# A graph network on one Trainium2 core: in the first edge sweep the rank row is loaded to one partition and spread by TensorE

## The chip, the cores and the metric

The kernel runs on one core of one Trainium2 chip, as a single launch. The metric is device time in microseconds (us) of that core, lower being better. TensorE is called PE in the profile, VectorE DVE, ScalarE ACT, GpSimd POOL and SyncE SP.

## The reference, cut to what matters

Four message-passing layers run over one graph of 6250 nodes with 128 features and 106250 edges, which are sorted by receiver (`dst`). Each is followed by a residual and a layer norm. Only the first layer is touched by the change:

```python
msg_in = jnp.concatenate([h[src], h[dst], w[:, None]], axis=1)
msg = jax.nn.relu(msg_in @ W1 + b1) @ W2 + b2
agg = jax.ops.segment_max(msg, dst, num_segments=n)
```

`h[src] @ W1[:128]` and `h[dst] @ W1[128:256]` are made once per node, as two tables in HBM; what is left for each edge is to fetch a row of each, add them and `w * W1[256]`, apply relu, multiply by `W2`, and take the maximum over the edges of one receiver.

## The kernel before, in words

An **edge sweep** goes over the edges in 208 blocks (`NB`) of 512 edges (`EB`), each of four tiles of 128 (`CT`). A **node phase** lies between two sweeps. `edge_phase(k)` is the first sweep with k = 1 and the two last with k = 4 and 5; `relation_phase` is the second (k = 2) and `attention_phase` the third. Only `edge_phase(1)` changes in what it does.

In the first sweep a block goes through the engines like this.

- **SP** (`load`) waits for a free `meta` buffer (`e_meta_free`, four buffers), then issues three transfers from HBM: `meta` (L1071), `recv` (L1076, 256 KB, the receivers' rows) and the edge weights (L1083, 2 KB). The `meta` transfer reads two rows of 512 bf16 values, the **rank row** (for each edge, which of the receiver rows in its tile it belongs to) and the **bar row** (what restarts the running maximum at a new receiver), and writes each of them to all 128 partitions: 256 KB.
- **POOL** (`gather`) issues four indirect transfers (L1040), one per tile, that fetch 128 rows of the joint table by `src`. It waits for a free gather buffer (`e_gath_free`) and for the store of half of that buffer's earlier content (`factor_out`).
- **DVE** (`same_receiver`, L1228) compares the rank row with a column of ranks and so makes the 0/1 matrix `same`, which spreads one receiver's row over its edges.
- **PE** (`senders`) waits for `recv`, `same` and the gather, then makes the sum in `pre_ps`: one matmul for the weight (L1120), and per tile one for the senders (L1123) and one for the receivers (L1124). `message` multiplies the hidden layer by `W2` (L1132), `turn_back` transposes the result of the scan (L1142).
- **ACT** (`hidden`) first issues the store of the factor half (L1168), then applies relu (L1171); it makes the gather's indices (L1156), and `keep_rows` frees `scan`, copies the transposed rows (L1184) and stores them (L1190).
- **DVE** (`reduce`, L1247) takes the running maximum over the block with `meta[s][:, 2, :]`, the bar row, and then frees the `meta` buffer, for which SP is waiting.

Each engine runs its pieces in an order written out by hand with `steps(engine, NB, SLOTS, (lag, piece), ...)`: in step i it does each piece for block i - lag, in the order given. Before, PE's step is `senders(i)`, `message(i-1)`, `turn_back(i-3)`; DVE's is `same_receiver(i)`, `reduce(i-2)`; ACT's is `hidden(i-4)`, `indices(i)`, `keep_rows(i-7)`; SP's is `load(i)`, which runs up to four blocks ahead.

The second sweep, `relation_phase`, already has the form that the change brings to the first: its `meta` rows go to one partition (L1292), `rank_row` on PE spreads the rank row with a bf16 matmul against a row of ones (L1315), and DVE compares out of PSUM (L1408).

Of the kernel before, what the change touches and what calls it, by code (L numbers as in the profile page):

```python
# [17 lines left out]
P = 128  # L18
# [5 lines left out]
EB = 512  # L24
CT = EB // P
NB = -(-E // EB)
# [8 lines left out]
SLOTS = 4  # L35
# [6 lines left out]
ALU = mybir.AluOpType  # L42
# [30 lines left out]
def gnn_program(nc, a, out):  # L73
# [8 lines left out]
    def sem(name):  # L82
        return ctx.enter_context(nc.semaphore(name))
# [4 lines left out]
    with ctx:  # L88
# [129 lines left out]
        t_er_free = sem("t_er_free"); t_cb_free = sem("t_cb_free"); t_gath_free = sem("t_gath_free")  # L218
        e_idx_free = sem("e_idx_free")
        e_rank = sem("e_rank"); e_rank_free = sem("e_rank_free")  # L220
        e_go = sem("e_go"); e_go_free = sem("e_go_free")

        def part(q, s, unroll, n):
# [781 lines left out]
        def edge_phase(k):  # L1005
# [2 lines left out]
            table, width = (joint_d, 2 * F) if k == 1 else (send_d, F)  # L1008
            landed = {1: joint, 2: factor}.get(k, gath)
            marks = {1: (1, 3), 2: (0, 2)}.get(k, (0, 1))  # L1010
            pre_ps, msg_ps, back_ps = bank[0:2], bank[2:4], bank[4:6]
            before = started["edge"]
            firsts_before, scatters = started["firsts"], started["scatter"]

# [2 lines left out]
            with nc.Block() as block:  # L1017
# [34 lines left out]
                @block.sync  # L1052
                def _(sp):
                    if expands:

                        sp.wait_ge(n_scat_all, 1)
                        sp.sem_inc(n_scat_all, -1)
                        sp.wait_ge(firsts_got, 16 * (firsts_before + TC))
                        by_tile = first_d.rearrange("(b p c) f -> b p c f", p=P, c=CT)
                        for c in range(TC):  # L1060
                            n = P if c < TC - 1 else TL
                            sp.dma_start(by_tile[c * P // CT:(c * P + n) // CT, 0, :, :], firsts[c // CT][0:n, c % CT, :]).then_inc(n_first_out, 16)
                        sp.wait_ge(n_first_out, 16 * TC)
                        sp.sem_inc(n_first_out, -16 * TC)

                    def load(q, s):

                        sp.wait_ge(e_meta_free, 1)
                        sp.sem_inc(e_meta_free, -1)
                        lo, hi = marks  # L1070
                        sp.dma_start(meta[s][:, lo:hi, :], meta_d[lo:hi, part(q, s, SLOTS, EB)].partition_broadcast(P)).then_inc(meta_in[s], 16)  # L1071
                        if expands:

                            sp.wait_ge(e_recv_free, 1)
                            sp.sem_inc(e_recv_free, -1)
                            sp.dma_start(recv[s][:, :, :], first_d[part(q, s, SLOTS, EB), :].rearrange("(p c) f -> p c f", c=CT)).then_inc(recv_in[s], 16)  # L1076
                            if k == 2:

                                sp.wait_ge(e_gath_free, 1)
                                sp.sem_inc(e_gath_free, -1)  # L1080
                                sp.dma_start(factor[s][:, :, :], factor_rows_d[part(q, s, SLOTS, EB), :].rearrange("(p c) f -> p c f", c=CT)).then_inc(factor_in[s], 16)
                            if k == 1:
                                sp.dma_start(wrow[s][:, :], weight_d[:, part(q, s, SLOTS, EB)]).then_inc(recv_in[s], 16)  # L1083

                    def store(q, s):

                        sp.wait_ge(e_rows, 1)
                        sp.sem_inc(e_rows, -1)
                        sp.dma_start(scan_d[part(q, s, SLOTS, EB), :].rearrange("(p c) f -> p c f", c=CT), rows[s][:, :, 0:F]).then_inc(stored[s], 16)

                    if expands:
                        steps(sp, NB, SLOTS, (0, load), *[(5, store)] * (k == 2))

                @block.tensor
                def _(pe):
                    def senders(q, s):
                        if expands:

                            pe.wait_ge(recv_in[s], 32 if k == 1 else 16)
                            pe.sem_inc(recv_in[s], -(32 if k == 1 else 16))  # L1100

                            pe.wait_ge(e_same, 1)
                            pe.sem_inc(e_same, -1)

                        pe.wait_ge(e_pre_free, 1)
                        pe.sem_inc(e_pre_free, -1)
                        if k == 2:

                            pe.wait_ge(factor_in[s], 16)
                            pe.sem_inc(factor_in[s], -16)  # L1110
                        else:
                            pe.wait_ge(gathered[s], (q + 1) * (16 * CT) + 16 * CT * rounds * before)
                        b, g = pre_ps[s % 2], landed[s]
                        if k >= 4:
                            for c in range(CT):
                                ins = pe.transpose(b[:, c * P:(c + 1) * P], g[:, c, 0:F], ident[:, :])  # L1116
                            ins.then_inc(e_pre, 1)
                            return
                        if k == 1:
                            pe.matmul(b[:, :], w1w[:, :], wrow[s][:, :], start=True, stop=False)  # L1120
                        for c in range(CT):
                            o = b[:, c * P:(c + 1) * P]
                            pe.matmul(o, g[:, c, 0:F], ident[:, :], start=k != 1, stop=False)  # L1123
                            ins = pe.matmul(o, recv[s][:, c, :], same[s % 2][:, c, :], start=False, stop=k != 1 or c == CT - 1)  # L1124
                        ins.then_inc(e_pre, 1)

                    def message(q, s):
                        pe.wait_ge(e_hid, 1)
                        pe.sem_inc(e_hid, -1)
                        pe.wait_ge(e_msg_free, 1)  # L1130
                        pe.sem_inc(e_msg_free, -1)
                        pe.matmul(msg_ps[s % 2][:, :], w2[:, :], hid[s % 2][:, :], start=True, stop=True).then_inc(e_msg, 1)  # L1132

                    def turn_back(q, s):

                        pe.wait_ge(e_scan, 1)
                        pe.sem_inc(e_scan, -1)

                        pe.wait_ge(e_back_free, 1)
                        pe.sem_inc(e_back_free, -1)  # L1140
                        for c in range(CT):
                            ins = pe.transpose(back_ps[s % 2][:, c * P:(c + 1) * P], scan[s % 2][:, c * P:(c + 1) * P], ident[:, :])  # L1142
                        ins.then_inc(e_back, 1)

                    steps(pe, NB, SLOTS, (0, senders), *[(1, message)] * (k == 1), (3 if expands else 2, turn_back))

                @block.scalar
                def _(act):
# [62 lines left out]
                def _(v):  # L1211
# [9 lines left out]

                    def same_receiver(q, s):

                        v.wait_ge(meta_in[s], 16)
                        v.sem_inc(meta_in[s], -16)
                        v.wait_ge(e_same_free, 1)
                        v.sem_inc(e_same_free, -1)
                        v.tensor_tensor(same[s % 2][:, :, :], meta[s][:, 1, :].rearrange("p (c e) -> p c e", e=P),  # L1228
                                        rank_cols[:, part(q, s, SLOTS, CT)].unsqueeze(2).to_broadcast([P, CT, P]), ALU.is_equal).then_inc(e_same, 1)

                    def reduce(q, s):
                        if k >= 4:

                            v.wait_ge(meta_in[s], 16)
                            v.sem_inc(meta_in[s], -16)
                        v.wait_ge({1: e_msg, 2: e_hid}.get(k, e_pre), 1)
                        v.sem_inc({1: e_msg, 2: e_hid}.get(k, e_pre), -1)
                        if k == 1:
                            v.sem_inc(e_hid_free, 1)
                        if k >= 4:  # L1240
                            v.sem_inc(e_gath_free, 1)
                            v.sem_inc(e_idx_free, 1)
                        v.wait_ge(e_scan_free, 1)
                        v.sem_inc(e_scan_free, -1)  # L1244
                        src = {1: msg_ps, 2: hid}.get(k, pre_ps)[s % 2][:, :]
                        go_on = meta[s][:, 2 if k == 1 else 0, :]
                        chain(v.tensor_tensor_scan(scan[s % 2][:, :], go_on, src, scan[1 - s % 2][:, EB - 1:EB],  # L1247
                                                   ALU.add if k == 1 else ALU.mult, ALU.max if k == 1 else ALU.add))
                        v.sem_inc({1: e_msg_free, 2: e_hid_free}.get(k, e_pre_free), 1)
                        v.sem_inc(e_meta_free, 1)  # L1250
                        v.sem_inc(e_scan, 1)
# [551 lines left out]
```

## Time and profile before

| | |
|---|---|
| three timed runs | 6587.62, 6593.26 (median), 6595.1 us |
| profiled execution | 6596.86 us, of which 6595.1 us are its span |
| busy shares of the span | PE 56%, PE weight load 43%, DVE 38%, ACT 21%, POOL 59% |
| first sweep | from 396 to 1530 us of the span |
| in the first sweep | PE 999, DVE 411, ACT 309, POOL 844 us busy of 1134; DMA share 0.94 |

Busy shares over the whole span say little here, since the six stages have different limits. The first sweep is one stage of some 1130 us, and the change is to be read from that stretch alone. The DMA share is the mean busy share of the core's 16 DMA engines. Indirect transfers are issued by POOL, and an issue counts as POOL's busy time.

### The profile page before, as it was taken

To read this page: it belongs to the slowest core of one execution; us is meant where nothing else is said; L and a number is where in the kernel's file an instruction comes from. 1 tells how busy PE (TensorE), PEld (TensorE's weight loads), DVE (VectorE), ACT (ScalarE), POOL (GpSimd) and SP (SyncE) were. 2 spreads that over 40 slices of the span, in tenths; PEclk is the share of its full clock that TensorE was granted. 3 is DMA by queue.
4 is the path that set the end of the run, shared out by engine and by line. 5 is a ranking of instruction groups with operands and counts; after the bars stand their busy time and mean duration, and the time that the engine had idled before them with its cause. 6 is when DMAs were issued, how large, how long until landed. Compare 5 with 4: busy or idle time off the path is not lost. (4 is left out here: it accounts for less than half of the span.)

```text
span 6595.1 us, 101052 instructions
## 1 busy us (share of the span) xinstructions
PE 3682.2 (56%) x19907; PEld 2827.0 (43%) x19907; DVE 2495.9 (38%) x4067; ACT 1392.2 (21%) x3059; POOL 3886.5 (59%) x3936
## 2 busy tenths in 40 slices
PE   1258888896587777636666564233333343333334
PEld 1145565564465555435555554123323332332332
DVE  4223333334344444525655555422222212222224
ACT  0012222222122232212222222111111111111111
POOL 0467777776200000667777774577777757777775
PEclk9679999998799999767878777555555565555556
DMA  9369999993355555256656563344544434444452
GB/s 343 123 193 293 291 296 292 298 297 105 122 182 182 186 182 171 81 124 171 168 156 168 156 169 103 92 126 125 127 126 125 126 86 126 125 127 126 125 127 75
DMA packets 1080339, 1090.67 MB, mean 165 GB/s; under 512 B 128353, under 2 KB 867622, under 8 KB 1076854
## 3 DMA queue, kind: packets, MB, share of 16 engines
q1 hardware_dynamic: 398532, 393.02, 20.3%
q10 hardware_dynamic: 546204, 390.09, 19.1%
q0 software_dynamic: 135456, 306.11, 18.5%
q14 instruction: 117, 0.96, 0.0%
q8 instruction: 30, 0.49, 0.0%
HBM read 662.62 MB, written 427.19 MB: 165 GB/s over the span
## 5 line engine op out<-in xcount | busy, mean ns | idle before, releaser
L1040 POOL DMA_INDIRECT gath<-sender_table,idx x1664 | 1657.6, 996 | 547.4 <-issue 376.0
L1247 DVE TENSOR_TENSOR_SCAN scan<-meta,scan,bank 128x512 f32<-128x512 bf16 x624 | 798.6, 1280 | 2086.1 <-DVEq L1244 2083.0
L1116 PE MATMUL bank<-ident,gath 128*128 128x128 f32 x1664 | 464.1, 434 | 1367.3 <-DMA gath<-sender_table,idx 1367.3
L1463 POOL DMA_INDIRECT gath<-attention_table,idx x832 | 852.3, 1024 | 349.3 <-issue 226.7
L1040 POOL DMA_INDIRECT gath<-joint_table,idx x832 | 850.3, 1022 | 273.6 <-issue 213.0
L1116 PEld LDWEIGHTS bank<-ident,gath 128*128 128x128 f32 x1664 | 297.7, 217 | 1533.4 <-DMA gath<-sender_table,idx 1533.4
L682 POOL COPY idx<-end_i 128x4 int32<-128x4 int32 (+1 forms) x65 | 13.5, 207 | 1040.5 <-POOLq L681 1040.3
L1184 ACT ACTIVATE rows<-bank 128x512 f32<-128x512 f32 x624 | 372.7, 597 | 1101.7 <-ACTq L1183 1059.1
L1142 PE MATMUL bank<-ident,scan 128*128 128x128 f32 x2496 | 570.1, 374 | 5.0 <-PEq L1140 5.0
L1142 PEld LDWEIGHTS bank<-ident,scan 128*128 128x128 f32 x2496 | 471.7, 203 | 132.0 <-issue 132.0
L1123 PE MATMUL bank<-ident,gath 128*128 128x128 f32 x1664 | 374.8, 310 | 0.0
L1329 PE MATMUL bank<-ident,gath 128*128 128x128 f32 x1664 | 350.5, 294 | 23.7 <-PEq L1325 12.0
L1124 PE MATMUL bank<-same,recv 128*128 128x128 f32 x1664 | 357.2, 300 | 0.0
L1514 PE MATMUL bank<-recv,same 128*128 128x4 f32 x1664 | 229.0, 261 | 222.8 <-PEq L1512 215.6
L1123 PEld LDWEIGHTS bank<-ident,gath 128*128 128x128 f32 x1664 | 279.3, 211 | 161.6 <-issue 161.6
L1514 PEld LDWEIGHTS bank<-recv,same 128*128 128x128 f32 x1664 | 223.4, 208 | 255.9 <-issue 255.9
L1120 PE MATMUL bank<-small,w1w 1*128 1x512 f32 x416 | 237.1, 650 | 165.3 <-DMA gath<-joint_table,idx 113.8
L1422 DVE TENSOR_TENSOR_SCAN scan<-bank,scan,hid 128x512 f32<-128x512 f32 x208 | 266.8, 1283 | 159.3 <-DVEq L1421 159.3
L1156 ACT ACTIVATE idx<-src_cols 128x4 int32 (+1 forms) x624 | 127.8, 205 | 876.9 <-ACTq L1194 772.5
L1171 ACT ACTIVATE hid<-bank,b 128x512 f32<-128x512 f32 x208 | 143.0, 687 | 739.8 <-ACTq L1170 667.0
L1329 PEld LDWEIGHTS bank<-ident,gath 128*128 128x128 f32 x1664 | 263.1, 199 | 80.9 <-issue 80.9
L1124 PEld LDWEIGHTS bank<-same,recv 128*128 128x128 f32 x1664 | 285.6, 215 | 0.0
(245 smaller groups left out, 6065.8 us busy)
## 6 DMA issues: line engine op xcount, KB each, us to landing
recv<-receiver_rows SPq DMA_DIRECT2D x624, 256.0 KB
scan_rows<-rows ACTq DMA_DIRECT2D x624, 256.0 KB
attention_scan_rows<-rows ACTq DMA_DIRECT2D x208, 264.0 KB
receiver_rows<-gath ACTq DMA_DIRECT2D x26, 2048.0 KB, 11.2
meta<-edge_meta SPq DMA_DIRECT2D x208, 256.0 KB
factor_rows<-gath ACTq DMA_DIRECT2D x208, 256.0 KB
gath<-factor_rows SPq DMA_DIRECT2D x208, 256.0 KB
scan_rows<-rows SPq DMA_DIRECT2D x208, 256.0 KB
```

The source lines that it names most:

```text
L1040: pool.indirect_dma_start(out=landed[s][:, c, 0:width], out_offset=None, in_=table[:, :], in_offset=bass.IndirectOffsetOnAxis(ap=idx[s][:, ...
L1116: ins = pe.transpose(b[:, c * P:(c + 1) * P], g[:, c, 0:F], ident[:, :])
L1120: pe.matmul(b[:, :], w1w[:, :], wrow[s][:, :], start=True, stop=False)
L1123: pe.matmul(o, g[:, c, 0:F], ident[:, :], start=k != 1, stop=False)
L1124: ins = pe.matmul(o, recv[s][:, c, :], same[s % 2][:, c, :], start=False, stop=k != 1 or c == CT - 1)
L1142: ins = pe.transpose(back_ps[s % 2][:, c * P:(c + 1) * P], scan[s % 2][:, c * P:(c + 1) * P], ident[:, :])
L1184: ins = act.activation(rows[s][:, :, 0:F], back_ps[s % 2][:, :].rearrange("p (c f) -> p c f", f=F), ACT.Copy)
L1247: chain(v.tensor_tensor_scan(scan[s % 2][:, :], go_on, src, scan[1 - s % 2][:, EB - 1:EB], ALU.add if k == 1 else ALU.mult, ALU.max if k = ...
L1329: pe.matmul(o, factor[s][:, c, :], ident[:, :], start=True, stop=False)
L1422: chain(v.tensor_tensor_scan(scan[s % 2][:, :], go_ps[s % 2][:, :], hid[s % 2][:, :], scan[1 - s % 2][:, EB - 1:EB], ALU.mult, ALU.add))
L1463: pool.indirect_dma_start(out=gath[s][:, c, :], out_offset=None, in_=att_d[:, :], in_offset=bass.IndirectOffsetOnAxis(ap=idx[s][:, c:c + 1 ...
L1514: ins = pe.matmul(er_ps[:, c * HEADS:(c + 1) * HEADS], same[s % 2][:, c, :], recv[s % SLOTS][:, c, 0:F:HID], start=True, stop=True)
```

## The change

The rank row no longer goes to all partitions. SP loads it to partition 0, in a transfer of its own of 1 KB, and the bar row in a second broadcast transfer of 128 KB with a semaphore of its own (`bar_in`). PE spreads the rank row into PSUM (banks 6 and 7, `rank_ps`) with one bf16 matmul per block, in front of `senders` of the block before, so that PE's other pieces come one step later. DVE compares out of PSUM, with the running maximum waiting for `bar_in`.

```diff
+        bar_in = [sem(f"bar_in{s}") for s in range(SLOTS)]
...
-                        sp.dma_start(meta[s][:, lo:hi, :], meta_d[lo:hi, part(q, s, SLOTS, EB)].partition_broadcast(P)).then_inc(meta_in[s], 16)
+                        sp.dma_start(meta[s][0:1, lo:lo + 1, :], meta_d[lo:lo + 1, part(q, s, SLOTS, EB)].unsqueeze(0)).then_inc(meta_in[s], 16)
+                        sp.dma_start(meta[s][:, lo + 1:hi, :], meta_d[lo + 1:hi, part(q, s, SLOTS, EB)].partition_broadcast(P)).then_inc(bar_in[s], 16)
...
+                    def rank_row(q, s):
+                        pe.wait_ge(meta_in[s], 16)
+                        pe.sem_inc(meta_in[s], -16)
+                        pe.wait_ge(e_rank_free, 1)
+                        pe.sem_inc(e_rank_free, -1)
+                        pe.matmul(rank_ps[s % 2][:, :], ones_row[:, :], meta[s][0:1, 1, :], start=True, stop=True).then_inc(e_rank, 1)
...
-                    steps(pe, NB, SLOTS, (0, senders), *[(1, message)] * (k == 1), (3 if expands else 2, turn_back))
+                    if expands:
+                        steps(pe, NB, SLOTS, (0, rank_row), (1, senders), (2, message), (4, turn_back))
+                    else:
+                        steps(pe, NB, SLOTS, (0, senders), (2, turn_back))
...
-                        v.wait_ge(meta_in[s], 16)
-                        v.sem_inc(meta_in[s], -16)
+                        v.wait_ge(e_rank, 1)
+                        v.sem_inc(e_rank, -1)
                         v.wait_ge(e_same_free, 1)
                         v.sem_inc(e_same_free, -1)
-                        v.tensor_tensor(same[s % 2][:, :, :], meta[s][:, 1, :].rearrange("p (c e) -> p c e", e=P),
-                                        rank_cols[:, part(q, s, SLOTS, CT)].unsqueeze(2).to_broadcast([P, CT, P]), ALU.is_equal).then_inc(e_same, 1)
+                        chain(v.tensor_tensor(same[s % 2][:, :, :], rank_ps[s % 2][:, :].rearrange("p (c e) -> p c e", e=P),
+                                              rank_cols[:, part(q, s, SLOTS, CT)].unsqueeze(2).to_broadcast([P, CT, P]), ALU.is_equal))
+                        v.sem_inc(e_rank_free, 1)
+                        v.sem_inc(e_same, 1)
...
+                        if k == 1:
+                            v.wait_ge(bar_in[s], 16)
+                            v.sem_inc(bar_in[s], -16)
```

## Rows read from the trace of the kernel before

**Rows 1.** Windows: busy us of each engine, PE clock, DMA share, GB/s.

```profile
600.00:800.00 200.00, 177.68 (x899) 117.99 (x898) 73.55 (x75) 55.13 (x111) 152.75 (x150) 0.93 0.95 294
2000.00:2600.00 600.00, 475.79 (x3071) 356.32 (x3070) 275.23 (x279) 179.88 (x280) 0.00 (x0) 0.97 0.59 183
```

**Rows 2.** Groups of instructions by line, first sweep, window 600 to 1400 us.

```profile
L1040 POOL DMA_INDIRECT gath<-joint_table,idx x600 | 614.1, 1024 | 187.4 <-issue 155.2 <-POOLq L1038 13.0 <-POOLq L1034 11.6
...
L1228 DVE TENSOR_TENSOR same<-meta,rank_cols 128x512 f32<-128x512 bf16 x150 | 104.1, 694 | 190.7 <-DVEq L1227 162.6 <-ACTq L1164 14.8 <-DVEq L1225 9.2
```

**Rows 3.** The page's costliest groups: the gathers of the whole first sweep.

```profile
L1040 POOL DMA_INDIRECT gath<-joint_table,idx x832 | 850.3, 1022 | 273.6 <-issue 213.0 <-POOLq L1038 32.6 <-POOLq L1034 16.2
```

**Rows 4.** Instructions of line 1040, first sweep, then last sweeps (ns: min/median/max).

```profile
L1040 POOL DMA_INDIRECT gath<-joint_table,idx x823: 992/998/1512, 399.5 to 1510.3; - x165
...
L1040 POOL DMA_INDIRECT gath<-sender_table,idx x1199: 992/997/1013, 4799.8 to 6466.8; - x200
```

**Rows 5.** Timeline: start, length; gathers of POOL beside comparisons of DVE.

```profile
405.99 1.19 POOL L1040 DMA_INDIRECT gath<-joint_table,idx  x1 [0.30 <-issue]
...
1013.56 0.69 DVE L1228 TENSOR_TENSOR same<-meta,rank_cols 128x512 f32<-128x512 bf16 x1 [1.46 <-DVEq L1227]
1013.72 1.40 POOL L1040 DMA_INDIRECT gath<-joint_table,idx  x1 [0.30 <-issue]
...
1508.92 1.09 POOL L1040 DMA_INDIRECT gath<-joint_table,idx  x1 [0.30 <-issue]
```

**Rows 6.** Waits, window 600 to 1400 us: engine, who for whom, us, times, longest.

```profile
PEld bank L1120 <- DMA gath<-joint_table,idx: 104.2, 91, 2.8
```

**Rows 7.** DMA queue of SP, window 600 to 1400 us: packets, MB, share.

```profile
q1 hardware_dynamic: 62471, 78.64, 31.6%
```

**Rows 8.** Timeline: one turn of a block, from senders to the next load.

```profile
1009.56 1.12 PE L1120 MATMUL bank<-small,w1w 1*128 1x512 f32 x2
...
1013.92 0.69 ACT L1171 ACTIVATE hid<-bank,b 128x512 f32<-128x512 f32 x1 [2.48 <-ACTq L1170]
...
1015.23 1.28 DVE L1247 TENSOR_TENSOR_SCAN scan<-meta,scan,bank 128x512 f32<-128x512 bf16 x1 [0.98 <-DVEq L1244]
...
1016.98 0.38 SPq L1071 DMA_DIRECT2D meta<-edge_meta  x1
```

**Rows 9.** Timeline: the first and the last pair of senders and load.

```profile
409.09 1.22 PE L1120 MATMUL bank<-small,w1w 1*128 1x512 f32 x1
...
417.77 0.40 SPq L1071 DMA_DIRECT2D meta<-edge_meta  x1
...
1500.61 0.69 PE L1120 MATMUL bank<-small,w1w 1*128 1x512 f32 x1
...
1507.71 0.38 SPq L1071 DMA_DIRECT2D meta<-edge_meta  x1
```

**Rows 10.** Timeline, second sweep: first and last load of rows, and PE behind it.

```profile
1724.18 0.73 SPq L1292 DMA_DIRECT2D meta<-edge_meta  x1
...
1726.37 0.58 PE L1315 MATMUL bank<-meta,ones_row 1*128 1x512 bf16 x1 [42.61 <-PEq L1314]
...
2609.83 0.63 SPq L1292 DMA_DIRECT2D meta<-edge_meta  x1
...
2611.92 0.37 PE L1315 MATMUL bank<-meta,ones_row 1*128 1x512 bf16 x1 [0.81 <-PEq L1314]
...
2612.38 0.46 PE L1329 MATMUL bank<-ident,gath 128*128 128x128 f32 x2
```

**Rows 11.** Timeline, first sweep: a comparison that waited for its broadcast rows.

```profile
1022.73 0.37 SPq L1071 DMA_DIRECT2D meta<-edge_meta  x1
...
1028.32 0.69 DVE L1228 TENSOR_TENSOR same<-meta,rank_cols 128x512 f32<-128x512 bf16 x1 [1.27 <-DMA meta<-edge_meta]
```

**Rows 12.** Instructions of line 1408, second sweep: the comparison out of PSUM.

```profile
L1408 DVE TENSOR_TENSOR same<-bank,rank_cols x104: 691/692/693, 1727.2 to 2604.3; 128x512 f32<-128x512 f32 x104
```

More of the change, by code:

```diff
@@ L1010, in edge_phase @@
             marks = {1: (1, 3), 2: (0, 2)}.get(k, (0, 1))
-            pre_ps, msg_ps, back_ps = bank[0:2], bank[2:4], bank[4:6]
+            pre_ps, msg_ps, back_ps, rank_ps = bank[0:2], bank[2:4], bank[4:6], bank[6:8]
             before = started["edge"]
```

## The prediction

> **What bounds the first sweep now.** I read the windows by stage first. In the steady part of the first sweep PE is busy 178 of 200 us, POOL 153, and the DMA engines 0.95 of the time [rows 1]. Three resources are near their end, so the busy shares do not name the bound. The groups by line do: between 600 and 1400 us POOL issues 600 gathers, 150 blocks, so a block takes 800 / 150 = 5.333 us; POOL's instructions are busy for 614.1 us and idle 187.4 [rows 2]. Nearly every gather has the same 0.30 us in front of it [rows 5], 180 us for 600, which is issue cost and no wait. Only some 6 of 800 us are left as waits for another engine. POOL's row of gathers is the bound.
>
> How low can it go? The median gather takes 998 ns [rows 4], so four of them with 0.30 each are 4 x 1.298 = 5.19 us per block. The step is 0.14 us longer. One part of that is in the gathers' own length: they average 1024 ns here, while in the last sweeps the longest of 1199 is 1013 [rows 4]. Over the sweep that is 832 x (1.022 - 0.998) = 20 us [rows 3, 4]. The timeline says where it lies. In the first sweep 82 of the 832 gathers last over 1.02 us (first and last: [rows 5]), and each begins just ahead of or inside a comparison L1228 on DVE, as at 1013.72, 0.16 us into one, with 1.40 us [rows 5]. None of the 669 gathers that begin away from one is long. So POOL is held by the comparison, not by the full DMA queues.
>
> The Trainium skill has a rule for this (page "SBUF — State Buffer", section "Who interferes with whom"): a DVE instruction with two SBUF inputs contends with a GpSimd instruction that reads SBUF, since its second input comes through the shared read interface; one with at most one SBUF input does not. The trace agrees as far as it goes. By that rule the 20 us go entirely once one input lies in PSUM.
>
> PE has some room: its first matmul of a block waits for the gather 104.2 us in 150 blocks [rows 6], 0.69 us each, so its own work is about 5.33 - 0.69 = 4.64 us.
>
> **The change, part by part.**
>
> Removed: 128 KB per block minus 1 KB of transfers. SP's queue moves 78.64 MB in 150 blocks [rows 7], 0.52 MB each, and each of the other two streams about as much, so some 8% of all bytes go. As DMA is not what the gathers wait for, this is worth nothing directly. It makes the queues shorter; the waits of POOL outside the steady part could shrink: 273.6 us idle over 832 gathers [rows 3] less 832 x 0.30 leaves 24 us, of which 6 are in the steady part [rows 2]. I count none of the other 18 us, and keep 5 of them for the range.
>
> The comparison: out of PSUM it takes 692 ns [rows 12] against 694 now [rows 2]. No cost. Its other effect is the gain above, if the mechanism is what I take it for: up to 20 us, or 0.10 us per block. The second sweep has no gathers beside its comparison, so no row shows this directly; the bounds are 0 and 20 us, and I take 20, because only gathers that meet L1228 are long, and the scans (one operand in PSUM) leave the others at 998 ns.
>
> PE's new matmul: in the second sweep `senders` begins 2612.38 - 2611.92 = 0.46 us behind the rank matmul [rows 10]. PE's work becomes 4.64 + 0.46 = 5.10 us, still below 5.19, with its room down from 0.69 us to 0.1. It is hidden behind POOL's gathers; without that cover it would cost 208 x 0.46 = 96 us.
>
> SP issues a fourth transfer, and the one-row form takes 0.63 us [rows 10] instead of 0.38; SP's four issues are about 2 us of a 5.3 us step. `recv` and the weights are issued about 1 us later; they have three steps. The running maximum waits for `bar_in`, issued just behind the rank row and needed more than two steps later. Neither is on the path.
>
> **The new wait** is what decides. `rank_row(b)` stands in front of `senders(b-1)` on PE and waits for a transfer that SP can issue only when `reduce(b-4)` has freed the buffer. Behind it on PE queue senders, message and turn_back; behind them ACT, and POOL, which needs a freed gather buffer. So there is a loop over two steps. Its links: from S, the start of `senders(m+1)`, at 1009.56, to relu at 1013.92, to ACT's `keep_rows`, which frees `scan`, to the running maximum of block m at 1015.23, to SP's next load at 1016.98 [rows 8]: 7.42 us. This is also the median over 204 pairs; their mean is 7.66 (first and last pair: [rows 9]), as some turns have a slower stretch of PE in them. That load is of block m+4, and its rank matmul stands ahead of `senders(m+3)`. With L from the issue to the rank matmul and the 0.46 us behind it, two steps need at least 7.42 (7.66) + L + 0.46. Before, the comparison, not PE, waited for this transfer, and `senders(b)` needed it three steps after: 7.42 + 5.59 [rows 11] + the comparison's 0.69 is 13.7 us against 3 x 5.33 = 16.0, hidden by over 2 us.
>
> L is not in the trace of this sweep. Nearest row: the second sweep, one-row transfer, 2.09 us at 2609.83; over all 208 the median is 2.11 and the mean 2.23 (first and last: [rows 10]). There the DMA share is 0.59 [rows 1]. Upper bound: the 256 KB broadcast of this sweep, 5.59 us [rows 11], which contains its own 256 packets and the tail of the transfer before it. I take 2.5: the transfer form of the lower row, plus 0.3 for queues that will be about 0.88 busy (0.95 less its 8%). The Trainium skill (page "DMA: Bandwidth & Descriptors", section "Anatomy of one DMA — SWDGE (gpsimd) path") speaks against hoping for more: about 2 us of a transfer are fixed, whatever its size. It gives that for the GpSimd path; 2.09 us here for SP's queue agrees, and with 2.0 the loop would give 4.9 to 5.1 us per step, no bound.
>
> With L = 2.5 the loop's step is (7.42 + 2.5 + 0.46) / 2 = 5.19 by the median turn and (7.66 + 2.5 + 0.46) / 2 = 5.31 by the mean one. At 2.23 it is 5.06 and 5.18. Below 5.19 POOL still sets the pace. In the timeline the slow turns stand behind PE's longer waits for a gather, and these get shorter when PE is nearly full, so I take 7.5: 5.23. Two loops that near to each other add a little of their jitter: 5.25 us.
>
> **Sum.** 208 x (5.333 - 5.25) = 17 us less. The profiled execution has 6596.86 us, 3.6 above the median of the three runs, so it would go to 6580, and the median of 6593.26 to 6576.
>
> **The rivals.**
>
> A. *POOL alone sets the pace*: L is near 2.2. The step is 5.19 to 5.21 and a few us of early waits go too: 208 x 0.13 = 27 plus up to 5, 6561 to 6570. For it: the second sweep's L hardly moves with its load. Chance 0.13.
>
> B. *The port is freed, the rank wait takes its place*: L about 2.6 with mean turns, (7.66 + 2.6 + 0.46) / 2 = 5.36, or the contention does not come from the second SBUF input. The step is 5.28 to 5.39: 6582 to 6605, about 6592. For it: two of today's steps less the turn, 10.67 - 7.66 = 3.0 us, is all the time that `senders(b-1)` now starts behind the issue of `meta(b)`, on average; with L + 0.46 = 3.06 about half of the blocks would be held. Chance 0.29.
>
> C. *The rank wait becomes the bound* (slower): it decides from L above 2.7 on (mean turn, 0.2% of the time being 13 us or 0.063 us per step). With L = 3.0 the step is (7.66 + 3.0 + 0.46) / 2 = 5.56, 208 x 0.227 = 47 us more, 6640; with 2.8, 5.46, 6620. For it: 0.9 busy queues, with 256 KB of `recv` issued one step earlier on the same queue; against it: that data has had nearly 5 us to drain. At the far bound, L = 5.59, the step would be 6.86 and the time 6910; I see no reason for it, as the rank row has one packet of its own. Chance 0.28.
>
> The forecast (5.21 to 5.27, 6573 to 6580) has 0.30.
>
> **How the numbers follow.** Time differences under about 0.2%, 13 us, cannot be told from no change. Faster: forecast and A, 0.43. Same: B, 0.29. Slower: C, 0.28. For 8 in 10 the range starts at the lower end of A, 6560, and goes up into C to L = 3.05, 6645. The forecast's own range is 6570 to 6580.
>
> **What would show it.** Gathers of line 1040 at a mean of 998 ns with none above 1.02 would show the port step right; long ones that still go with the comparison would show it wrong. The median from the rank row's issue to its matmul is L when PE waits there; PE's idle in front of the rank matmul, and whether POOL now waits for L1034 or L1038, show which loop binds. The steady step (POOL's 600 gathers) should be 5.25 us. I am wrong if L is above 2.7, or if the long gathers stay.

## The result and the profile after

The changed kernel takes 6635.44 us (median of 4 runs, 6632.59 to 6640.45) beside 6591.85 us for the kernel before (4 runs): ratio 1.0067, 95% interval 1.005 to 1.0085. It is slower by 44 us. I had forecast 6576 us, faster. Rival C, "the rank wait becomes the bound", named 6640.

The last running maximum of the first sweep starts at 1573.6 us instead of 1525.1, 48.5 us later, while what follows takes 5061.3 us instead of 5070.0. That remainder, the span less the start of that instruction, lies between 5061.3 and 5078.3 us in the profiled executions of these two kernels and of the eight below that ran where the kernel before takes some 6600 us, so it is variation, and the loss is that of the first sweep.

Windows from 600 to 1400 us, the kernel before and the changed one, columns as in [rows 1]:

```profile
600.00:1400.00 800.00, 714.48 (x3589) 475.54 (x3588) 294.71 (x299) 222.70 (x448) 612.88 (x600) 0.92 0.95 295
600.00:1400.00 800.00, 722.24 (x3530) 465.55 (x3528) 278.03 (x282) 210.62 (x424) 563.93 (x566) 0.92 0.87 255
```

The DMA share went from 0.95 to 0.87, which was expected, but POOL does 566 gathers instead of 600, and POOL and the DMA engines both have time to spare. PE is busy 722.24 / 141.5 = 5.10 us per block, as the prediction had it (though from 4.76 before, not 4.64), while a block takes 5.65 us. No engine's own work is as long as the step, which is what a wait that goes around in a loop looks like; the experiments below test whether it is one.

Groups by line, window 600 to 1400 us, changed kernel (beside [rows 2]):

```profile
L1041 POOL DMA_INDIRECT gath<-joint_table,idx x566 | 564.4, 997 | 236.8 <-issue 150.5 <-POOLq L1039 65.7 <-POOLq L1035 9.5
...
L1135 PE MATMUL bank<-meta,ones_row 1*128 1x512 bf16 x141 | 53.2, 377 | 63.0 <-PEq L1134 61.4 <-PEq L1132 1.1
```

The step is 4 x 800 / 566 = 5.65 us, where it was 5.33. POOL's gathers average 997 ns instead of 1024, and its idle time holds 236.8 - 566 x 0.30 = 67 us of real waits, most of them for line 1039, the store of the factor rows. PE waits 61.4 us in front of the new matmul (L1135). The comparison out of PSUM takes 692 ns.

The page's group and the instructions of the gathers (beside [rows 3, 4]):

```profile
L1041 POOL DMA_INDIRECT gath<-joint_table,idx x832 | 829.7, 997 | 342.6 <-issue 219.0
```

```profile
L1041 POOL DMA_INDIRECT gath<-joint_table,idx x823: 992/998/1011, 399.4 to 1558.7; - x165
```

The longest gather was 1512 ns and is 1011: the long ones are gone, all 82, and 850.3 - 829.7 = 20.6 us with them. The port step of the prediction is right to within 1 us, and nothing of it reaches the time.

In the window 600 to 1400 us SP's queue moved 78.64 MB in 150 blocks [rows 7] and moves 55.94 MB in 141, 0.40 MB each instead of 0.52.

The timeline through one turn of the loop, changed kernel (beside [rows 8]):

```profile
1264.01 1.09 PE L1122 MATMUL bank<-small,w1w 1*128 1x512 f32 x2
...
1268.26 0.69 ACT L1184 ACTIVATE hid<-bank,b 128x512 f32<-128x512 f32 x1 [3.52 <-ACTq L1183]
...
1269.65 1.28 DVE L1266 TENSOR_TENSOR_SCAN scan<-meta,scan,bank 128x512 f32<-128x512 bf16 x1 [2.71 <-DVEq L1263]
...
1271.43 0.25 SPq L1072 DMA_DIRECT2D meta<-edge_meta  x1
...
1274.08 1.00 POOL L1041 DMA_INDIRECT gath<-joint_table,idx  x1 [1.86 <-POOLq L1039]
...
1275.14 0.37 PE L1135 MATMUL bank<-meta,ones_row 1*128 1x512 bf16 x1 [1.86 <-PEq L1134]
...
1275.78 0.69 PE L1122 MATMUL bank<-small,w1w 1*128 1x512 f32 x1 [0.26 <-PEq L1108]
```

From one `senders` at 1264.01 to SP's issue at 1271.43 are the same 7.42 us as in [rows 8]. The row's matmul follows 3.71 us behind the issue, PE having stood idle for 1.86, and the `senders` of two blocks on begins at 1275.78, 11.77 us after the first. POOL, which had run ahead, has waited 1.86 us of its own until 1274.08, for a store of factor rows that ACT issues only when PE is through with `senders`.

In 100 of the 184 blocks from the 24th on PE had been idle over 0.2 us in front of the rank matmul, so that L, the time from the issue to the matmul, is the landing and some 0.2 us in which PE takes the semaphore. Their means, from the starts in the timeline: turn 7.77 us, L 2.86, from the matmul to `senders` 0.53; together 11.16 for two steps, 5.58 for one. In the other 84 PE came too late to wait. That was not of PE's own making alone: 70 of them stand right behind a block in which PE did wait. PE's busy time also differs from step to step: its median is 4.74 us, but in 40 of 183 steps it is over 5.3 us, in slower stretches of the PE clock (from 556.9 to 561.0 us, for one, the granted clock is 0.66). In the step before one of those 40 PE had been idle for 1.10 us on average, before the others for 0.41 us.

### The profile page after: what moved, and what is told of

It reads as the page before. It is cut to its first block and busy times, and to the rows that moved or that the text cites. A ratio compares the mean times of both kernels' runs of the same rounds, so it can differ in the third digit from the quotient of the medians.

```text
span 6634.9 us, 103382 instructions
## 1 busy us (share of the span) xinstructions
PE 3734.3 (56%) x20115; PEld 2836.3 (43%) x20115; DVE 2492.7 (38%) x4067; ACT 1392.0 (21%) x3059; POOL 3866.8 (58%) x3936
## 5 line engine op out<-in xcount | busy, mean ns | idle before, releaser
L1041 POOL DMA_INDIRECT gath<-joint_table,idx x832 | 829.7, 997 | 342.6 <-issue 219.0
L1441 DVE TENSOR_TENSOR_SCAN scan<-bank,scan,hid 128x512 f32<-128x512 f32 x208 | 266.8, 1283 | 159.1 <-DVEq L1440 159.1
L1780 DVE TENSOR_TENSOR_SCAN scan<-bank,scan,hid 128x512 f32<-128x512 f32 x208 | 265.8, 1278 | 19.2 <-DVEq L1779 19.0
```

The lines of the kernel that those rows point to most:

```text
L1041: pool.indirect_dma_start(out=landed[s][:, c, 0:width], out_offset=None, in_=table[:, :], in_offset=bass.IndirectOffsetOnAxis(ap=idx[s][:, ...
L1441: chain(v.tensor_tensor_scan(scan[s % 2][:, :], go_ps[s % 2][:, :], hid[s % 2][:, :], scan[1 - s % 2][:, EB - 1:EB], ALU.mult, ALU.add))
L1780: chain(v.tensor_tensor_scan(scan[s % 2][:, :], fac_ps[s % 2][:, :], hid[s % 2][:, :], scan[1 - s % 2][:, EB - 1:EB], ALU.mult, ALU.add))
```

## The experiments

Twelve kernels ran, four on each of three chips; the first letter of a label stands for the chip. The kernel before takes 7800.69 us on chip `e`, 6603.8 us on `f` and 6599.26 us on `g`. Ratios are against the kernel before on the same chip. All four experiments of chip `e` were repeated on `f` or `g`, since the result above is of a chip where that kernel takes some 6600 us.

**The rank row one step earlier**, `e1_early_rank`, then `f1_early_rank`:

```diff
+                    def load_rank(q, s):
+                        lo, hi = marks
+                        sp.wait_ge(e_row_free, 1)
+                        sp.sem_inc(e_row_free, -1)
+                        sp.dma_start(meta[s][0:1, lo:lo + 1, :], ...).then_inc(meta_in[s], 16)
...
-                        sp.dma_start(meta[s][0:1, lo:lo + 1, :], ...).then_inc(meta_in[s], 16)
...
-                        steps(sp, NB, SLOTS, (0, load), *[(5, store)] * (k == 2))
+                        steps(sp, NB, SLOTS, (0, load_rank), (1, load))
...
+                        v.sem_inc(e_row_free, 1)
```

The first removed line stood in `load`, the last added one stands in `same_receiver`, behind the comparison. The new semaphore starts with four credits, one for each `meta` buffer.

> The changed kernel, but SP loads the rank row of a block one step earlier, against a credit of its own that DVE gives back after the comparison, so that it no longer waits for the running maximum four blocks back. Theory 'loop' (the wait of PE for the rank row, issued only when reduce has freed the meta buffer, sets the pace): PE's idle in front of the rank matmul goes to nearly nothing, POOL is the bound again with gathers of 0.998 us, the step is 5.20 to 5.25 us, and the time is 6560 to 6575. Rival 'PE' (the added matmul, 0.46 us per block, fills PE): nothing changes, 6630 to 6640. Rival 'stores' (POOL waits for the factor stores because they got slower): POOL's waits for line 1039 stay at some 65 us in 800, 6625 or more.

Measured on the chip with 7800 us: 7823.06 us, ratio 1.0037 (1.0022 to 1.0051): slightly slower. There the sweep waits for the stores with or without the change (see `e3_cols_in_psum`).

> The changed kernel with the rank row loaded one step earlier against its own credit, again, on the chip of this call. Where the kernel before takes about 6590 us: theory 'loop' 6560 to 6575, POOL at 5.20 to 5.25 us per block; rival 'PE' 6630 to 6640; rival 'stores' 6625 or more with POOL's waits for line 1039 at 65 us in 800. Where it takes 7800 us POOL waits for the stores in any case, and all theories give 7790 to 7830.

Measured: 6577.05 us, ratio 0.9962 (0.9947 to 0.9976). Groups by line and waits, window 600 to 1400 us:

```profile
L1041 POOL DMA_INDIRECT gath<-joint_table,idx x610 | 608.4, 997 | 192.3 <-issue 154.1 <-POOLq L1039 16.2 <-POOLq L1035 14.0
...
L1140 PE MATMUL bank<-meta,ones_row 1*128 1x512 bf16 x152 | 58.4, 384 | 0.0
```

```profile
PEld bank L1127 <- DMA gath<-joint_table,idx: 75.7, 94, 2.7
```

610 gathers are 5.246 us per block, POOL's real waits are down to 192.3 - 610 x 0.30 = 9 us, and PE waits for gathers again (the last row, beside [rows 6]) and is not idle at all in front of its rank matmul (L1140). PE and DVE do the same work in the same order as in the changed kernel and the same transfers are made; SP takes the row's credit elsewhere and issues the row ahead of the other three. That takes 70 us less than the changed kernel takes on this chip (below). The rivals "PE" and "stores" fall.

In the sweep by itself the last running maximum starts at 1497.9 us, 27 us before that of the kernel before (profiled executions on two chips). By the starts of `senders` 17 of them are gained in the last 183 steps (960.1 us instead of 977.1) and 11 in the first 24 (124.6 instead of 135.3), where the prediction had seen 18 us of other waits and had counted none.

**The changed kernel beside them**, `f0_changed`, no edit:

> The changed kernel itself, to have its ratio on the chip of this call. Where the kernel before takes about 6590 us, 6635 (0.7% slower) again. Where the DMA engines are slower, as in the call before (kernel before at 7800 us, 215 GB/s in the first sweep, POOL waiting 220 us in 800 for the factor stores), L and the two-step loop are longer too but so is everything else: theory 'loop' expects it slower by 0.2 to 1%.

Measured: 6646.75 us, ratio 1.007 (1.0052 to 1.0087). The loss of the result, 0.67%, comes again on this chip.

**The rank row last**, `e4_rank_last`, then `f3_rank_last`: the changed kernel, with the line that issues the rank row moved behind the edge weights.

```diff
-                        sp.dma_start(meta[s][0:1, lo:lo + 1, :], ...).then_inc(meta_in[s], 16)
                         sp.dma_start(meta[s][:, lo + 1:hi, :], ...).then_inc(bar_in[s], 16)
...
                                 sp.dma_start(wrow[s][:, :], ...).then_inc(recv_in[s], 16)
+                                sp.dma_start(meta[s][0:1, lo:lo + 1, :], ...).then_inc(meta_in[s], 16)
```

> The changed kernel, with the rank row issued as the last of SP's four transfers instead of the first, about 2.0 us later; nothing else differs. Theory 'loop': two steps get longer by 2.0 us wherever the rank wait sets the pace, so the step goes from 5.63 to some 6.4 to 6.6 us, 150 to 208 us more: 6785 to 6845. Rival 'PE' (PE's work sets the pace and the rank row has time to spare): at most 30 us more, 6635 to 6665.

Measured: 7990.11 us, ratio 1.026 (1.023 to 1.0291), 189 us more.

> The changed kernel with the rank row issued last of SP's four transfers, again, on the chip of this call. Where the kernel before takes about 6590 us: theory 'loop' some 2.0 us more on two steps, the step at 6.4 to 6.6 us, 6785 to 6845; rival 'PE' at most 6665.

Measured: 7079.44 us, ratio 1.0734 (1.0705 to 1.0762): 433 us more than the changed kernel, more than twice what theory "loop" had said. Groups, windows and waits, 600 to 1400 us:

```profile
L1041 POOL DMA_INDIRECT gath<-joint_table,idx x421 | 419.8, 997 | 381.1 <-POOLq L1039 263.4 <-issue 95.9 <-ACTq L1175 14.2
```

```profile
600.00:1400.00 800.00, 605.23 (x2612) 396.05 (x2611) 206.98 (x210) 156.44 (x315) 419.18 (x421) 0.83 0.66 190
```

```profile
1807.20:1812.00 4.80, 4.58 (x13) 2.77 (x14) 0.69 (x1) 0.00 (x0) 2.95 (x3) 0.55 0.80 224
```

The step is 7.60 us, and PE waits 187.8 us in front of its rank matmul, up to 4.8 us at a time. Three things make up the miss of the size. The three issues ahead of the row cost 1.6 us (the 10% value of the turn is 8.90 instead of 7.32). The row also landed later: L is 3.92 instead of 2.86 where PE was idle before it, now that 384 KB stand in front of it on its queue. And the granted clock is 0.83 in the window instead of 0.92: the last row is a stretch right behind 4.20 us in which PE stood idle, and there the clock is 0.55, that is, nearly all of it at the lower level. In a quarter of the turns relu now starts over 6.5 us behind `senders`, where the median is 4.3. How much of the miss is due to each was not measured by itself. The direction and the mechanism hold: nothing but the issue of a row of 1 KB was made later.

**One operand in PSUM, nothing else**, `e3_cols_in_psum`, then `f2_cols_in_psum`, on the kernel before:

```diff
+                    def columns(q, s):
+                        act.activation(bank[6 + s % 2][:, 0:CT], rank_cols[:, part(q, s, SLOTS, CT)], ACT.Copy).then_inc(e_cols, 1)
...
+                        v.wait_ge(e_cols, 1)
+                        v.sem_inc(e_cols, -1)
                         v.tensor_tensor(same[s % 2][:, :, :], meta[s][:, 1, :].rearrange("p (c e) -> p c e", e=P),
-                                        rank_cols[:, part(q, s, SLOTS, CT)].unsqueeze(2)...
+                                        bank[6 + s % 2][:, 0:CT].unsqueeze(2)...
```

> The kernel before, with one thing of the change alone: the comparison has one operand in PSUM. Here it is the column of ranks, which ACT copies (128x4) into PSUM for each block; the rank row is broadcast by the transfer as before. If POOL's long gathers come from two SBUF operands of the comparison, the gathers average 0.998 us, none is over 1.02, and the time falls by 20 us to about 6572 (6568 to 6580). If they come from the output or from DVE at all, they stay and the time is 6590 to 6596.

Measured on the chip with 7800 us: 7803.64 us, ratio 1.0007 (0.9992 to 1.0022), no change. Groups and windows, 600 to 1400 us, of that run:

```profile
L1040 POOL DMA_INDIRECT gath<-joint_table,idx x440 | 438.7, 997 | 363.1 <-POOLq L1038 221.5 <-issue 125.0 <-ACTq L1162 11.7
```

```profile
600.00:1400.00 800.00, 607.06 (x2646) 395.61 (x2646) 218.37 (x222) 184.53 (x444) 438.72 (x440) 0.82 0.73 217
```

The gathers are at 997 ns here too, but on this chip the sweep moves 217 GB/s and not 295, POOL waits 221.5 us for its stores, and a shorter gather only waits longer.

> The kernel before with the column of ranks read out of PSUM, again, on the chip of this call. Where the kernel before takes about 6590 us, POOL sets the pace and the 20 us of the long gathers are gained: 6568 to 6580. If shorter gathers only wait longer for the stores, 6585 to 6595. The gathers average 0.997 us in either case, as they did in the call before.

Measured: 6587.65 us, ratio 0.9982 (0.9972 to 0.9992), 16 us less in the medians and 12 by the ratio. The group, 600 to 1400 us, and the gathers of the whole sweep (ns: min/median/max):

```profile
L1040 POOL DMA_INDIRECT gath<-joint_table,idx x609 | 607.5, 998 | 194.0 <-issue 157.1 <-POOLq L1038 16.4 <-POOLq L1034 13.4
```

```profile
L1040 POOL DMA_INDIRECT gath<-joint_table,idx x832: 992/998/1016, 388.9 to 1493.7; - x167
```

The rank row comes from SBUF as before, the output goes where it went, and the second SBUF operand is gone (at the price of a small copy on ACT, 177 ns): that takes the long gathers away. The gain is a little short of 20 us, POOL's waits having grown from 7 to 194.0 - 609 x 0.30 = 11 us. Read literally, 6587.65 lies in the range of the other branch, 6585 to 6595; but the kernel before takes 6604 on this chip and not 6590, and 0.9982 of 6590 is 6578, in the first one.

**The matmul alone**, `e2_matmul_alone`, then `g0_matmul_alone`, on the kernel before:

```diff
+                    def spread_alone(q, s):
+                        if isinstance(q, int) and q * SLOTS + s == 0:
+                            return
+                        pe.matmul(bank[6 + s % 2][:, :], ones_row[:, :], meta[(s - 1) % SLOTS][0:1, 1, :], start=True, stop=True)
...
-                    steps(pe, NB, SLOTS, (0, senders), ...
+                    steps(pe, NB, SLOTS, *[(0, spread_alone)] * (k == 1), (0, senders), ...
```

> The kernel before, with one bf16 matmul of ones_row against a meta row added per block at the head of PE's step, into a bank that nobody reads; no wait, no transfer and no order is changed, and the result is not used. It prices the PE work of the change alone. Rival 'PE': most of the loss is here, 6620 to 6640. Theory 'loop': PE had 0.69 us of room per block and 0.46 are taken, so POOL still sets the pace, 6590 to 6605.

Measured on the chip with 7800 us: 7809.15 us, ratio 1.0012 (0.9996 to 1.0029).

> The kernel before, with one bf16 matmul of ones_row against a meta row added per block at the head of PE's step, into a bank that nobody reads; no wait, no transfer and no order is changed, and the result is not used. On a chip where the kernel before takes about 6600 us. Theory 'loop': PE had 0.69 us of room per block, 0.46 of it are taken, POOL still sets the pace: within 10 us of the kernel before. Rival 'PE work': a good part of the 44 us of the change is here, 20 us or more.

Measured: 6600.32 us, ratio 0.9998 (0.9986 to 1.001). PE's wait for gathers, 600 to 1400 us, beside [rows 6]:

```profile
PEld bank L1120 <- DMA gath<-joint_table,idx: 80.0, 84, 2.7
```

104.2 us of waiting became 80.0; the matmul went into PE's room and cost nothing that can be measured (the interval is from 9 us less to 7 us more).

**The wait alone**, `g3_wait_alone`, on the kernel before:

```diff
+                        sp.dma_start(meta[s][0:1, 0:1, :], meta_d[1:2, part(q, s, SLOTS, EB)].unsqueeze(0)).then_inc(row_in[s], 16)
                         sp.dma_start(meta[s][:, lo:hi, :], ...).then_inc(meta_in[s], 16)
...
+                    def wait_row(q, s):
+                        pe.wait_ge(row_in[s], 16)
+                        pe.sem_inc(row_in[s], -16)
...
+                        steps(pe, NB, SLOTS, (0, wait_row), (1, senders), (2, message), (4, turn_back))
```

> The kernel before, plus the wait of the change alone: SP first issues a transfer of the rank row to one partition (into a row that nobody reads), and PE waits for it at the head of its step, with the lags of the changed kernel; no matmul is added, and the comparison reads the broadcast row as before. Theory 'loop': two steps need 7.66 + L + 0.1 with L about 3.0 at this DMA load; 5.4 to 5.6 us per block, 15 to 50 us more than the kernel before. Rival 'PE work' (the wait costs only because PE has no room for the matmul): within 10 us of the kernel before.

Measured: 6672.4 us, ratio 1.0103 (1.0073 to 1.0133): 73 us more, above the 15 to 50 expected. Group and waits, 600 to 1400 us:

```profile
L1041 POOL DMA_INDIRECT gath<-joint_table,idx x561 | 569.4, 1015 | 231.2 <-issue 146.2 <-POOLq L1039 62.4 <-POOLq L1032 13.1
```

```profile
PE bank L1122 <- PEq L1108: 117.5, 95, 3.1
```

No matmul, and the comparison untouched, yet this is more than the whole loss of the change. PE stands 117.5 us in front of `senders`. The row names only the last thing that PE's sequencer did (L1108), but in all 132 of the 184 blocks from the 24th on in which PE was idle over 0.2 us, PE took the semaphore of the row 0.50 to 0.73 us before `senders` began, so that the row was what it had waited for. The means of these blocks fit the loop: turn 7.82 us, from the row's issue to `senders` 3.37, together 11.19 for two steps.

**senders before the rank row**, `g2_rank_after_senders`, on the changed kernel:

```diff
-                        steps(pe, NB, SLOTS, (0, rank_row), (1, senders), (2, message), (4, turn_back))
+                        steps(pe, NB, SLOTS, (1, senders), (0, rank_row), (2, message), (4, turn_back))
```

> The changed kernel with one line changed: PE does senders(i-1) first and rank_row(i) behind it, so that senders no longer stands behind the wait for the rank row. Theory 'loop': the rank row lands some 10.3 to 10.7 us after the start of senders two blocks back, about when these senders begin, and they last 2.9 us, so that the wait is covered; POOL sets the pace at 5.20 to 5.27 us per block, 20 to 30 us less than the kernel before. Rival 'PE work': as the changed kernel, 40 us more than before.

Measured: 6566.93 us, ratio 0.9945 (0.9925 to 0.9966), 32 us less than the kernel before, a little more than the 20 to 30 expected. Groups and windows, 600 to 1400 us:

```profile
L1041 POOL DMA_INDIRECT gath<-joint_table,idx x611 | 609.5, 997 | 190.8 <-issue 155.2 <-POOLq L1039 17.3 <-POOLq L1035 14.6
...
L1135 PE MATMUL bank<-meta,ones_row 1*128 1x512 bf16 x153 | 59.4, 388 | 0.0
```

```profile
600.00:1400.00 800.00, 756.67 (x3821) 470.57 (x3820) 301.49 (x306) 227.16 (x459) 609.43 (x611) 0.99 0.91 276
```

The rank matmul follows the first matmul of its step by some 3.0 us, with no idle time in front; by then the row has landed. The step is 5.24 us, and the turn, 7.66 us on average before, is 7.45: PE's busy time is over 5.3 us in only 5 of 183 steps. This is the lowest ratio of all versions, by the swap of two entries of one line, but its interval overlaps that of `f1_early_rank`, and in the sweep the two are equal: its last running maximum starts at 1499.8 us, the other's at 1497.9.

**The bytes back**, `g1_bytes_back`, on the kernel of the early rank row:

```diff
+                        sp.dma_start(meta[s][:, 0:1, :], meta_d[0:1, part(q, s, SLOTS, EB)].partition_broadcast(P)).then_inc(bar_in[s], 16)
...
-                            v.wait_ge(bar_in[s], 16)
+                            v.wait_ge(bar_in[s], 32)
```

> The kernel of the early rank row (6577 us where the kernel before took 6604) with a second broadcast transfer of 128 KB per block, of a row that nobody reads, so that the bytes of the kernel before are moved again. It splits the gain of the early rank row. If the gain is the port alone, it stays where it is, within 6 us of 27 us less than the kernel before. If the fewer bytes have a share, the kernel loses up to 15 us of it.

Measured: 6602.03 us, ratio 1.0001 (0.9988 to 1.0013). All of the gain is gone, more than the 15 us that were expected at most. Group and windows, 600 to 1400 us:

```profile
L1041 POOL DMA_INDIRECT gath<-joint_table,idx x601 | 599.5, 998 | 201.9 <-issue 153.7 <-POOLq L1039 21.1 <-POOLq L1035 13.7
```

```profile
600.00:1400.00 800.00, 747.78 (x3763) 490.43 (x3763) 295.92 (x301) 223.46 (x450) 598.44 (x601) 0.93 0.96 296
```

The gathers stay at 998 ns, but POOL now waits 201.9 - 601 x 0.30 = 22 us, and the DMA engines are at 0.96 and 296 GB/s, as in the kernel before. With all the bytes and a PE that has less room, the port's 20 us are handed back as waits. So the 128 KB are worth something here: about 25 us between this kernel and `f1_early_rank`, measured on two chips, half of them (14 us by the starts of `senders`) in the first 24 steps. The added transfer is also a fifth issue for SP in each block, which was not tested apart from its bytes.

## Why the prediction was wrong, point by point

**What bounds the sweep: half right.** POOL's row of gathers did bound it. But the DMA engines at 0.95 were a second limit close behind, and I wrote that fewer bytes are "worth nothing directly". `g1_bytes_back` against `f1_early_rank` shows some 25 us. The limit shows only together with the added matmul: `f2_cols_in_psum`, with all the bytes and without it, has 609 gathers in 800 us, and `f1_early_rank`, with fewer bytes, 610, both close to the 616 that gathers of 1.298 us would give.

**The port: right.** 20 us of long gathers were expected to go and 20.6 went. `f2_cols_in_psum` shows that the second SBUF operand is the cause. This is the Trainium skill's rule (page "SBUF — State Buffer", section "Who interferes with whom"), and both kernels agree with it, with a longest gather of 1011 ns in the changed one and 1016 ns in `f2_cols_in_psum`, instead of 1512.

**The comparison and the matmul: right in effect.** The comparison takes 692 ns. The matmul was hidden in PE's room, as `g0_matmul_alone` shows by its ratio of 0.9998. Its price was put too high: where PE does not wait, `senders` begins 0.23 us (median) behind it in the changed kernel, and 0.48 us (median) only where PE had waited. The SP issue of the row is shorter too than I took it to be from the second sweep, 0.25 us instead of 0.63.

**The new wait: the right place, the wrong size.** This is the step that failed. The loop over two steps was laid out with its links, and each of them is there in the trace after. Three of its terms were too small. L: 2.5 taken, 2.86 measured (mean where PE was idle before it); I had added 0.3 us to the second sweep's row for queues that are 0.88 busy, and 0.6 to 0.75 was due. The turn: I took 7.5 us because the slow turns should become rarer. They did not: 7.65 over all blocks, 7.77 where the loop held. Each wait for the row is idle time of PE, and slow stretches stand behind such idle time; only in `g2_rank_after_senders`, where PE never waits for the row, did the mean turn fall, to 7.45. From matmul to `senders`: 0.53 instead of 0.46. With these, (7.77 + 2.86 + 0.53) / 2 = 5.58 us instead of 5.23. The last 0.06 to 5.64, the mean step, come from the 84 blocks in which PE was too late to wait, with two-step sums of 11.44 us. What all this made of the time: the sweep ended 48.5 us later, where I had forecast 17 us earlier.

With the turn's mean from before and no hope in it, (7.66 + 2.86 + 0.46) / 2 = 5.49 would have given 33 us more, rival C. I preferred the value of the turn that let the forecast stand; the trace of before held the better one.

**The weights.** C, "it decides from L above 2.7 on", had 0.28. It happened as described, with POOL waiting for the store that ACT issues behind a late PE. `g3_wait_alone` (73 us), `f1_early_rank` (the same work without the wait, 70 us less than the changed kernel on its chip) and `g2_rank_after_senders` (80 us less than the changed kernel, by the two ratios 0.9945 and 1.007 to 1.0067) show it from three sides. What they do not settle is the exact split of the 44 us, and why the wait alone cost more at the full bytes than the whole change did at fewer. A longer landing under the full bytes may be part of that, but is not shown: from the row's issue until PE takes its semaphore it is 2.80 us in `g3_wait_alone`, 2.65 in the changed kernel and 2.75 in `f0_changed` (means where PE was idle), so that two executions of one kernel differ nearly as much. What is plain is that PE waits more often there, in 132 of 184 blocks instead of 100.

**The sum.** 208 x (5.65 - 5.33) = 67 us by the window's steps is more than the 48.5 us between the sweeps' ends. By the starts of `senders` the last 183 steps took 1032.5 us instead of 977.1, 5.64 and 5.34 each, which is 55 us, and the first 24 took 131.9 instead of 135.3, since the kernel before was slowed there by waits of its own. That rival C named 6640 us, 5 us from the result, is in part luck: it reckoned 208 steps and took L = 3.0, where L was 2.86 and the turn longer.

## What to carry to other kernels

When a transfer is replaced by a small one plus a matmul, the bytes and the matmul are the small questions; ask in whose queue the wait for it now stands, and what else is behind it there. A wait at the head of an in-order engine's step closes a loop with whatever frees the buffer: write the loop out, add the landing time under the load of that very stage and the mean of the turn, not its median, and divide by the steps it spans. If it comes near the present step, put the wait behind the work that does not need it, or load one step earlier, before anything else.

## What the runs showed of the hardware that was not expected

- From the issue of a transfer of one row of 1 KB to the matmul that waits for it are 2.11 us (median) at a DMA share of 0.59 [rows 1, 10], 2.76 (median; mean 2.86) at 0.87, and 3.92 behind 384 KB on its own queue at 0.66. Its size was the same in all of them.
- The granted PE clock of the window 600 to 1400 us is 0.92 in the kernel before and in the changed one alike, so the clock by itself does not tell them apart. PE is idle there for 0.57 and 0.56 us per step. The clock is 0.94 in `f1_early_rank` and 0.99 in `g2_rank_after_senders`, in neither of which PE waits for the rank row, and 0.83 in `f3_rank_last`, where it waits most (1.84 us per step). Why `g2_rank_after_senders` has more clock than `f1_early_rank` at nearly the same idle time, 0.30 and 0.33 us per step, stays open. The clock has two levels, 2.4 and 1.2 GHz; in `f3_rank_last` the pair of matmuls of L1122 takes 1.02 us at a clock of 1.00, and 2.06 us right behind the idle 4.20 us.
- One of the chips took 7800 us for the kernel that takes 6600 on the others, and `e3_cols_in_psum` moved 217 GB/s in the first sweep there, where the kernel before moves 295. There the order of the bounds is another: POOL's waits for the stores come first, and neither the port (ratio 1.0007) nor the matmul (1.0012) can be measured.
